# One load buffer more, weight casts moved to VectorE, and feed-forward groups quantized in pairs

## What is computed

```python
n = layernorm(x)
# one summary vector per 64 tokens: the mean of n over the chunk that ends there
summary = chunk_means(n)                         # (2, 128, 1024)
q = n @ Wq + bq                                  # 16 heads of 64
k = summary @ Wk + bk;  v = summary @ Wv + bv
scores = where(ends <= position, q @ k.T / 8, -inf)
x = x + softmax(scores) @ v @ Wo + bo

def block_quant(v):      # blocks of 32 along the last axis share an exponent
    scale = exp2(floor(log2(max(amax, 2**-126))) - 3)
    return round(v / scale) * scale
h = block_quant(layernorm(x)) @ block_quant(w_fc).T + b_fc      # 1024 -> 4096
x = x + block_quant(gelu(h)) @ block_quant(w_proj).T + b_proj   # 4096 -> 1024
```

## Time and profile before

| | |
|---|---|
| median of 3 runs | 3278.35 us (3278.29 to 3280.05) |
| the profiled execution's own time | 3275.63 us |
| its span on the slowest core | 3274.1 us |
| busy in the span: PE, DVE, ACT, POOL | 36%, 40%, 15%, 1% |
| summary stage | 0 to about 456 us |
| keys and values | to about 512 us |
| weight stage | to about 1064 us |
| attention | to about 1850 us |
| feed-forward stage | to 3274 us |

### The profile page before, as it was taken

How to read it: one execution, slowest core, us unless ns; L and a number is a source line. 1 busy time by engine, 2 the same in 40 slices (tenths; PEclk the granted TensorE clock), 3 DMA queues, 4 the chain that set the end, 5 groups by cost and what they waited for, 6 DMA issues and landing times.

```text
span 3274.1 us, 18464 instructions; the slowest of 8 cores (3262.4 to 3274.1 us)
## 1 busy us (share of the span) xinstructions
PE 1170.8 (36%) x5088; PEld 481.2 (15%) x5088; DVE 1322.9 (40%) x2809; ACT 475.8 (15%) x786; POOL 40.0 (1%) x60
## 2 busy tenths in 40 slices
PE   1111121111111332333322355455555555555546
PEld 0000010000001111111111122122211212122212
DVE  2333314666655142321324244444444444444443
ACT  0000001111111100101001022222121212121221
POOL 0000000000000000000000000000000000000000
PEclk9999995555555655566555676776777777777677
DMA  3222232112111302122020100000000000000000
GB/s 58 35 36 39 39 50 60 54 56 71 64 64 52 64 2 76 26 64 39 13 77 13 51 13 0 13 13 13 13 13 13 13 13 13 13 13 13 1 13 13
DMA packets 38405, 106.62 MB, mean 33 GB/s; under 512 B 5520, under 2 KB 5536, under 8 KB 36256
## 3 DMA queue, kind: packets, MB, share of 16 engines
q0 software_dynamic: 19392, 37.77, 7.1%
q1 hardware_dynamic: 18912, 67.68, 6.1%
HBM read 126.42 MB, written 16.78 MB: 44 GB/s over the span
## 4 chain that ended last, share of the span: by engine, by line
DVE 35%; PE 28%; DMA 13%; issue 11%; ACT 10%; DVEq 1%; SPq 0%; ACTq 0%; POOLq 0%
PE psC L937 9%; PE psE L233 5%; DMA xsq<-xseq 5%; DVE hqT L239 3%; DVE hqb L223 2%; DVE hbuf L220 2%; DVE wstr L540 2%; DVE qa_amax L462 2%; DMA wbuf<-wq_in 2%; DMA x2r<-xmid_scr 2%; DVEq L975 1%; DVE ebuf L239 1%; DVE bnscr L303 1%; ACT L180 1%; ACT L912 1%
## 5 line engine op out<-in xcount | busy, mean ns | idle before, releaser
L937 PE MATMUL psC<-wpjTq,hqT 128*128 128x512 bf16 x1024 | 366.5, 533 | 60.4 <-DVE hqT L239 60.4
L233 PE MATMUL psE<-ident,wqnat 128*128 128x128 bf16 x512 | 74.8, 300 | 476.6 <-DVE qa_e L481 390.6
L233 PE MATMUL psE<-ident,hqb 128*128 128x128 bf16 x512 | 69.8, 284 | 340.6 <-DVE hqb L223 279.8
L346 PE MATMUL psA<-xsq,patt 128*128 128x512 bf16 x64 | 37.5, 585 | 370.5 <-DVE meanb L343 370.5
L937 PEld LDWEIGHTS psC<-wpjTq,hqT 128*128 128x128 bf16 x1024 | 124.2, 127 | 280.0 <-issue 250.4
L912 ACT ACT_TABLE_LOAD x64 | 82.1, 1283 | 536.5 <-DVE hqT L239 400.7
L918 DVE TENSOR_REDUCE qa_amax<-hbuf 128x32 f32<-128x1024 f32 x64 | 78.1, 1220 | 162.5 <-ACT hbuf L912 162.5
L303 DVE BATCH_NORM_STATS2 bnscr<-xsq 128x6 f32<-128x512 bf16 x64 | 44.4, 694 | 226.1 <-DMA xsq<-xseq 221.3
L239 DVE CAST hqT<-psE 128x512 bf16<-128x512 f32 x128 | 88.5, 692 | 102.5 <-PE psE L233 102.5
L891 PE MATMUL psB<-wfcTq,xqfm 128*128 128x512 bf16 x256 | 115.6, 452 | 14.2 <-DVE xqfm L239 14.2
L233 PEld LDWEIGHTS psE<-ident,wqnat 128*128 128x128 bf16 x512 | 44.5, 127 | 507.2 <-issue 507.2
(11 more groups left out here) (215 smaller groups left out, 1967.8 us busy)
## 6 DMA issues: line engine op xcount, KB each, us to landing
xsq<-xseq POOLq DMA_DIRECT2D x32, 512.0 KB, 5.3
wstr<-wfc_in SPq DMA_DIRECT2D x32, 512.0 KB, 3.6
wstr<-wpj_in SPq DMA_DIRECT2D x16, 1024.0 KB, 4.9
xring<-xown SPq DMA_DIRECT2D x16, 512.0 KB, 5.8
wbuf<-wq_in POOLq DMA_DIRECT2D x8, 1024.0 KB, 8.2
wbuf<-wo_in POOLq DMA_DIRECT2D x8, 1024.0 KB, 8.1
xmid_scr<-xmid_t SPq DMA_DIRECT2D x16, 512.0 KB, 2.7
x2r<-xmid_scr SPq DMA_DIRECT2D x16, 512.0 KB, 4.1
```

What stands on the lines that cost most here:

```text
L233: E.matmul(d, s, ident[:, :], start=True, stop=True),
L937: S.op("tensor", lambda E, c_=c, cc=cl, cjj=cj, s_=gs: E.matmul(psC[:, cc:cc + 512], hqT[:, 1024 * s_ + 128 * cjj:1024 * s_ + 128 * cjj + ...
```

## The change

Three edits. The summary stage gets a third buffer, `xsq2`, and its loop body is cut into load, statistics and windows, which are emitted in another order. The cast of the weight stage's transposes goes to DVE. In the feed-forward stage the scaling of 1024 columns in the front goes to DVE, and the four groups are worked off in two pairs: gelu of both, block maxima of both, one `quant_consts` with 64 blocks, then passes, transposes and fc2 of the one and of the other; the front stands behind the two gelus of the first pair; `p2_fc1(t, 2)` is emitted behind fc2 of the first pair.

```diff
--- before.py
+++ after.py
@@ -154,6 +154,7 @@
         wqnat = sbp("wqnat", [128, 4096], BF16)
         xsq0 = sbp("xsq0", [128, 2 * D], BF16)
         xsq1 = sbp("xsq1", [128, 2 * D], BF16)
+        xsq2 = sbp("xsq2", [128, 2 * D], BF16)
 
         psA = psb("psA", [128, 1024])
         psB = psb("psB", [128, 1024])
@@ -286,18 +287,22 @@
 
         xs_view = xseq.rearrange("(c p) f -> p c f", p=128)
         NCH = 32
-        for ch in range(NCH):
-            buf = xsq0 if ch % 2 == 0 else xsq1
-            if ch >= 2:
-                S.wait_at("gpsimd", "PE", S.c("PE"))
-            xs_sem = "XS0" if ch % 2 == 0 else "XS1"
+        xsqs = [xsq0, xsq1, xsq2]
+
+        def xs_dma(ch):
+            buf = xsqs[ch % 3]
+            xs_sem = ["XS0", "XS1", "GE"][ch % 3]
             S.op("gpsimd",
                  lambda E, b=buf, c0=ch * 2: E.dma_start(
                      out=b.ap().rearrange("p (t f) -> p t f", f=D),
                      in_=xs_view[:, c0:c0 + 2, :]),
                  inc=xs_sem, amt=16)
-            lg_after = S.c(xs_sem)
-            S.wait_at("vector", xs_sem, lg_after)
+            return xs_sem, S.c(xs_sem)
+
+        def xs_stats(ch, sem_tot):
+            buf = xsqs[ch % 3]
+            xs_sem, tot = sem_tot
+            S.wait_at("vector", xs_sem, tot)
             for tt in range(2):
                 t = ch * 2 + tt
                 S.op("vector", lambda E, b=buf, o=tt: E.bn_stats(
@@ -327,8 +332,9 @@
             a_sl3 = a_seq.ap().rearrange("p (t one) -> p t one", one=1)[:, ch * 2:(ch + 1) * 2, :]
             S.op("vector", lambda E, a3=a_sl3, m3=mean_sl, o=am_sl3: E.tensor_tensor(
                 out=o, in0=a3, in1=m3, op=ALU.mult), inc="VE")
-            ve_now = S.c("VE")
-            S.wait_at("tensor", xs_sem, lg_after)
+
+        def xs_windows(ch):
+            buf = xsqs[ch % 3]
             for tt in range(2):
                 t = ch * 2 + tt
                 ncols = 2 if t == 63 else 3
@@ -353,6 +359,18 @@
                     psD[:, 0:1], p[:, :], meanb[:, :],
                     start=False, stop=False), inc="PE")
                 S.wait_at("vector", "PE", S.c("PE"))
+
+        sems_ch = {}
+        sems_ch[0] = xs_dma(0)
+        sems_ch[1] = xs_dma(1)
+        for ch in range(NCH + 1):
+            if ch < NCH:
+                xs_stats(ch, sems_ch[ch])
+            if ch >= 1:
+                xs_windows(ch - 1)
+                if ch + 1 < NCH:
+                    S.wait_at("gpsimd", "PE", S.c("PE"))
+                    sems_ch[ch + 1] = xs_dma(ch + 1)
 
         S.op("tensor", lambda E: E.matmul(psA[:, 0:512], zeros_b[:], mask_sb[:, 0:512],
                                           start=False, stop=True))
@@ -553,14 +571,14 @@
                            lambda j0, jn, h_=n: wfcTq.ap().rearrange(
                                "p (j r) -> p j r", r=HID)[:, j0:j0 + jn,
                                                           128 * h_:128 * h_ + 128],
-                           8, evac_eng="scalar")
+                           8, evac_eng="vector")
             else:
                 h_, hf = n // 2, n % 2
                 transpose8(lambda j, b=base: wqnat[:, b + 128 * j:b + 128 * j + 128],
                            lambda j0, jn, hh=h_, f_=hf: wpjTq.ap().rearrange(
                                "p (j r) -> p j r", r=D)[:, 16 * f_ + j0:16 * f_ + j0 + jn,
                                                         128 * hh:128 * hh + 128],
-                           16, evac_eng="scalar")
+                           16, evac_eng="vector")
 
         NJOB = len(jobs)
         wf_totals[0] = job_dma(0)
@@ -860,11 +878,11 @@
             S.wait_at("vector", "VE", S.c("VE"))
             S.op("vector", lambda E: E.tensor_scalar(out=nam2c[:], in0=nam2c[:], scalar1=-1.0,
                                                      scalar2=None, op0=ALU.mult), inc="VE")
-            w("scalar", "VE")
-            S.op("scalar", lambda E, b=buf: E.activation(
-                out=xln2[:, :], in_=b[:, :], func=ACT.Identity, scale=a2c[:, :],
-                bias=nam2c[:, :]), inc="AE")
-            w("vector", "AE")
+            S.wait_at("vector", "VE", S.c("VE"))
+            S.op("vector", lambda E, b=buf: E.tensor_scalar(
+                out=xln2[:, :], in0=b[:, :], scalar1=a2c[:, :], scalar2=nam2c[:, :],
+                op0=ALU.mult, op1=ALU.add), inc="VE")
+            S.wait_at("vector", "VE", S.c("VE"))
             o = 96
             v3 = xln2.ap().rearrange("p (b e) -> p b e", e=32)
             S.op("vector", lambda E, v=v3, o_=o: E.tensor_reduce(
@@ -903,25 +921,35 @@
                 d[:, 512:1024], ones_row[0:1, :], bfc_r[0:1, g_ * D + 512:g_ * D + 1024],
                 start=False, stop=True), inc="PE")
 
-        def p2_back(t):
-            for g in range(4):
-                dst = psA if g % 2 == 0 else psB
+        def p2_gelu(t, g):
+            dst = psA if g % 2 == 0 else psB
+            gs = g % 2
+            w("scalar", "PE")
+            S.wait_at("scalar", "VE", S.c("VE"))
+            S.op("scalar", lambda E, d=dst, s_=gs: E.activation(
+                out=hbuf[:, s_ * D:(s_ + 1) * D], in_=d[:, :], func=ACT.Gelu), inc="AE")
+
+        def p2_pair(t, pair, do_front):
+            g0, g1 = 2 * pair, 2 * pair + 1
+            p2_gelu(t, g0)
+            p2_fc1(t, g1)
+            p2_gelu(t, g1)
+            if do_front:
+                p2_front(t + 1)
+            w("vector", "AE")
+            for gi, g in enumerate((g0, g1)):
                 gs = g % 2
-                w("scalar", "PE")
-                S.wait_at("scalar", "VE", S.c("VE"))
-                S.op("scalar", lambda E, d=dst, s_=gs: E.activation(
-                    out=hbuf[:, s_ * D:(s_ + 1) * D], in_=d[:, :], func=ACT.Gelu), inc="AE")
-                if g < 3:
-                    p2_fc1(t, g + 1)
-                w("vector", "AE")
                 hg = hbuf.ap()[:, gs * D:(gs + 1) * D].rearrange("p (b e) -> p b e", e=32)
-                S.op("vector", lambda E, v=hg: E.tensor_reduce(
-                    out=qa_amax[:, 0:32], in_=v, axis=AXX, op=ALU.max,
+                S.op("vector", lambda E, v=hg, o=32 * gi: E.tensor_reduce(
+                    out=qa_amax[:, o:o + 32], in_=v, axis=AXX, op=ALU.max,
                     apply_absolute_value=True), inc="VE")
-                S.wait_at("vector", "VE", S.c("VE"))
-                quant_consts(32, qa_amax[:, 0:32], qa_e[:, 0:32], qa_s0[:, 0:32],
-                             qa_s[:, 0:32], qa_m[:, 0:32], qa_eb[:, 0:32])
-                ebg = qa_eb.ap()[:, 0:32].unsqueeze(2).broadcast_to([128, 32, 32])
+            S.wait_at("vector", "VE", S.c("VE"))
+            quant_consts(64, qa_amax[:, 0:64], qa_e[:, 0:64], qa_s0[:, 0:64],
+                         qa_s[:, 0:64], qa_m[:, 0:64], qa_eb[:, 0:64])
+            for gi, g in enumerate((g0, g1)):
+                gs = g % 2
+                hg = hbuf.ap()[:, gs * D:(gs + 1) * D].rearrange("p (b e) -> p b e", e=32)
+                ebg = qa_eb.ap()[:, 32 * gi:32 * gi + 32].unsqueeze(2).broadcast_to([128, 32, 32])
                 qg = hqb.ap().rearrange("p (b e) -> p b e", e=32)
                 S.wait_at("vector", "PE", S.c("PE"))
                 quant_apply(hg, hg, qg, ebg)
@@ -944,6 +972,13 @@
                             psC[:, cc:cc + 512], ones_row[0:1, :], bpj_r[0:1, cc:cc + 512],
                             start=False, stop=True),
                             inc="PE" if half == 1 else None)
+            if pair == 0:
+                S.wait_at("tensor", "AE", S.c("AE"))
+                p2_fc1(t, 2)
+
+        def p2_back(t, do_front):
+            p2_pair(t, 0, do_front)
+            p2_pair(t, 1, False)
             w("vector", "PE")
             oslot = t % 2
             buf = x2r0 if t % 2 == 0 else x2r1
@@ -960,9 +995,7 @@
         p2_front(0)
         for t in range(NT):
             p2_fc1(t, 0)
-            if t + 1 < NT:
-                p2_front(t + 1)
-            p2_back(t)
+            p2_back(t, t + 1 < NT)
 
         S.wait_at("sync", "ST0", 16 * (NT // 2))
         S.wait_at("sync", "ST1", 16 * (NT // 2))
```

## The result

The changed kernel took 3180.83 us (median of 8 runs, 3178.8 to 3183.5), the kernel before 3279.03 (8 runs): a ratio of 0.970, interval [0.969, 0.971], 98 us less. The prediction was 3264, so the sign was right and the size was not: its range of all ended at 3226. The spread of the 8 runs is 5 us.

A forecast was written before the change was run, and what follows sets the result against it. No engine is busy throughout, so chains of hand-overs bound each stage. Loads -4, weight casts -3 and feed-forward -7 sum to -14: 3261.6 us for the profiled execution, 3264 for the median; own range 3243 to 3271, of all 3226 to 3294.

The forecast's parts named there:

- (3): Feed-forward tile, first pair: fc2(0) takes 5.7 us to 41.3, then group 1's transposes and casts 2.8 to 44.1.
- (4): Feed-forward tile: fc2(1) 5.5 us, with 2 us lost to the clock, fc1(2) done at 53.8, fc1(3) at 57.9.
- (5): Feed-forward tile, second pair: fc2(2) from 72.9 takes 5.7 us, transposes 2.8, then 6.3; next add at 87.7 against 88.7.
- Loads, -4: Summary stage: 30 loads stay exposed at 14.0 us a chunk; only the start gains, -4 us, bounds -6 and 0.
- Weight casts, -3: Weight stage: casts on DVE change short jobs by -0.14 us, long by +0.02; -3 us taken, upper bound +5.
- (1): Feed-forward tile's start: fc1(0), fc1(1), gelu(1), front's Ln at 10.4 us, normalization on DVE 0.8; front ends at 23.2.
- (2): Feed-forward tile, reductions and constants for 64 columns: L220 of group 0 at 29.9 us, fc2(0) starts at 35.6.
- First and last tile: Feed-forward stage's ends: first tile's front ends 3.5 us later; last tile takes 75.1 against 71.64, +3.5.
- Rival (a): Feed-forward: the clock holds through the pause within a pair, 14 x 3.9 us less, total 3209; chance 0.12.
- Rival (e): Feed-forward: switching ACT's table costs more than its load, so fewer switches save 88 us more, total 3176; chance 0.02.

## Why the prediction was wrong, step by step

The steps that failed are (3), (4) and (5), and in them one kind of term: the lengths of fc2's bursts. They were given 5.7, 5.5, 5.7 and 6.3 us (the last to the add) and measured 4.94, 3.45, 4.73 and 4.53. The order of the chain, its waits and its other terms came out as forecast. Times are counted from the add at 2357.01, as the prediction counts from its own add.

- *Loads, -4:* the period stood as forecast; the 4 us were not seen in the time (+0.7 us by the medians, interval -1 to +5). The traces show most of them in the stage itself: its last window starts at 449.2 to 450.4 us in six kernels with this edit and at 452.4 to 453.7 in three without (means of the eight cores). This lead of about 3 us is lost again later; where is open.
- *Weight casts, -3:* both chains came out within 0.01 us; the kernel with this edit alone gained 6.5 (3 to 10), and its weight stage is 6.5 shorter on average. So -3 was too small: the distance from one short job to the next fell by 0.20 us on average (9.39 to 9.19), not by the 0.14 of the one job that was cut up.
- *Steps (1) and (2)* held: the front's Ln at 10.50 (10.4), scaling 0.81 (0.8), front's end 23.35 (23.2), L221 of group 0 at 29.86 (29.9), fc2(0) at 35.61 (35.6).
- *Step (3):* fc2(0) took 4.94, not 5.7, transposes 2.66, not 2.8: 0.9 less. The 5.7 was the mean over all four groups of before. A burst in this place took 5.3 to the end of its last matmul already there (5.23 in the row), 5.1 to PE's next work, and it still takes 5.3. The 5.7 was the wrong average to take; that part of the 0.9 is no gain of the change.
- *Step (4), "the open price", failed in size:* fc2(1) and fc1(2) were given 5.5 and 4.2; it was 3.45 and about 4.2, all at the full clock. That is 2.1 less. The price set a loss of 2 us to the clock behind a pause of 2.8 us; in 28 of the 32 pairs of this trace there was none.
- *Step (5):* fc2(2) took 4.73 (5.7) and the transposes 2.66 (2.8), and the last burst to the add 4.53 (6.3): 2.9 less. L221 to fc2(2) took 6.11, not 5.8, 0.3 more.
- *Sum of a tile:* 0.9 + 2.1 + 2.9 - 0.3 = 5.6 or so under the forecast's 87.7, and it is 82.09. The 5.9 of the first three are bursts and transposes at a higher clock than was assumed, not other operations that were costed wrongly; some 1.3 of it (fc2(0) and fc2(2) at 5.7, where 5.1 stood in their place) could have been read from the trace of before. The mean of the 14 full tiles is 82.45.
- *First and last tile:* the last took 75.35 (75.1 forecast). The first was given +3.5; from the first load of x2r (1847.19 before, 1842.35 after) to the first add it took 108.7 us before and 104.6 after.

Rival (a) gave the right outcome for nearly all second bursts and 3209, still too much, since it kept 5.7 for the first bursts, and since the first tile took 4 us less than before where +3.5 was given. Rival (e) gave 3176, the nearest number, for a reason that the runs don't bear out: the table loads did fall from 128 to 64, but the steps that contain them, (1) and (2), came out right within 0.15 us with a switch that costs its 1.28 us and nothing more, and filler on PE, which leaves every table load in place, moved the time by 63 us. The drain behind a table load that the Trainium skill states (ScalarE: Activation LUTs, What ACT_TABLE_LOAD costs) is not seen in this kernel.

That the length of the pause alone does not decide is shown: the same pause of 2.65 us went both ways in one tile, and 65 us between scaling on ScalarE and on VectorE shrank to 2 when PE was kept busy. That a longer pause costs is shown too (59.7 us, and all 32 second bursts slow behind 5.3 us). The prediction priced the clock by the pause. What it left out is that the two bursts of a pair go together: behind 2.65 us, when the clock rises late in the first, it is down again at the start of the second. The rows show this and not why; that the moment at which a burst comes decides it is the likely reading, as a shift of 0.45 us ahead of the bursts changed the outcome in 20 of the 32 pairs. The tile times also jump. In the changed kernel, in the one with its feed-forward stage alone, and in the three with a delay, all full tiles of the slowest core lie within 0.5 us of 82, 85.4, 88.7 or 92.2 us. A tile's delay of 0.45 us came out as over 3 in 13 of the 14 tiles with the scaling on ScalarE. Where fc1 comes early or filler was added, the tiles lie closer and the jumps are not seen so clearly (77.7 to 79.5 us with fc1 early). The Trainium skill (TensorE: Matmul & The Clock Gate, Part 1: The HAM clock gate) says of the start of a kernel that the count of slow matmuls varies from run to run with the phase; no run here tests that start, and inside this loop the opposite shows. Tile by tile the eight cores of the changed kernel have the same times within 0.25 us, but for two tiles that jumped on some cores only (to 85.3 on seven cores and on one). The series is again the same in the kernel with the feed-forward stage alone and in the one with the loads ahead, whose stage starts 168 us earlier. So the rhythm comes from the loop and not from the moment at which its stage starts.

That the changed kernel's delays happened to fit, while those with the scaling on ScalarE did not, could not have been read from the trace of before. In that the size of the gain is luck: with the scaling left on ScalarE the rest of the change gives 31 us and not 98. What could be read was that the clock is worth up to 3 us in each burst, and the range reached only halfway into rival (a).

Left open: how much of the gain of the changed kernel would stay if its tile were a little longer or shorter in another way; only two lengths of delay were tried. Filler between the transposes alone, without the matmuls ahead of them, was not tried either.

## What to carry to other kernels

Where matmuls come in bursts with light stretches between, read each burst in its own place and not as an average, price it at both levels of the clock and keep both ends in the range; here an edit of half a microsecond elsewhere moved more than half of the pairs of bursts from one to the other. Keep PE busy through the light stretches, between transposes that wait for casts as well as ahead of them: matmuls ahead alone did little, both together made the bursts even, and then half a microsecond more cost half a microsecond again. In this kernel a buffer more was worth nothing until the load was issued ahead of the work that it should hide behind: that order was worth 166 us, the buffer without it none. Work that is moved into idle time can still be waited for, where a wait takes in all that an engine was given: that cost 4.8 us a tile with fc1 early.

## What the runs showed of the hardware

- The granted clock fell at the end of a stretch in which PE was busy with transposes for 0.77 of 3.00 us and which began 1.8 us behind 6.8 us of dense matmuls (filler ahead alone).
- Behind the same pause of 2.65 us the second burst of a pair ran at the full clock 38 times and at the lower one at first 26 times, always by whether the first burst had taken at most 5.9 us or at least 6.2 (changed kernel, and the one with the scaling on ScalarE).
- Adding 114 matmuls a tile whose result is not read made the kernel 63 us faster, on all 8 cores (spans of 3098.1 to 3111.1 us against 3169.1 to 3180.8).
- Four matmuls of 512 columns fitted at the full clock between two groups of transposes for nothing: from group to group it is 1.33 us in the changed kernel (2397.56 to 2398.89) and 1.33 with them (2372.85 to 2374.18).
